# A graph transformer's edge stage: the running maximum moved from TensorE and DVE to DVE alone, q fetched three quads in front, sums added half a quad later

## The chip, the cores and the metric

The kernel runs on one core of one Trainium2 chip. The metric is the device time of one execution in microseconds. Engines: TensorE (PE), VectorE (DVE), ScalarE (ACT), GpSimd (POOL) and SyncE (SP), each with a queue of its own that runs in order; they meet in semaphores. POOL's gathers and scatters are indirect DMAs whose descriptors POOL makes itself; SP issues the plain ones.

## The reference

Two layers of a heterogeneous graph transformer on 6250 nodes, 100000 edges sorted by destination, 8 heads of 16, 16 node types and 32 edge types; then a projection, a residual and a layer norm. What matters here is the step over the edges:

```python
kw = kT[src, :, etype]                       # rows of a table with one entry per (node, edge type)
m = vT[src, :, etype]
a = jnp.einsum('ehd,ehd->eh', kw, q[dst]) * pri[:, etype].T / SQRT_D
amax = jax.ops.segment_max(a, dst, num_segments=n)
ex = jnp.exp(a - amax[dst])
att = ex / jax.ops.segment_sum(ex, dst, num_segments=n)[dst]
hag = jax.ops.segment_sum((m * att[:, :, None]).reshape(-1, H * HS), dst, num_segments=n)
```

## The kernel before, in words

A layer has a stage that builds (`fused`) and one over the edges (`attend`). The first makes, for each tile of 128 nodes, q, k and v and from them `relation_table`, 32 rows of 256 words (key and value) a node, and stores it in HBM. Before it in the first layer, a preparation sorts the nodes by type, spreads the edges over slots, and stores the per-slot flags (`segment_flags`, -1e30 at a segment's edge and 0 elsewhere) and the destination places (`edge_places`).

The edge stage works on 26 blocks of 32 slots; a slot holds 128 edges (one a partition) of one destination tile of 128 nodes. Four slots are a quad, so a block has 8 quads, and each engine runs a loop of one `step` per quad. What a quad X goes through, in steps:

- POOL gathers its rows, 4 indirect DMAs of 128 rows of 1 KB (L795), into a ring of three blocks. Two waits hold it back: TensorE's sums of the quad 24 places before must be done, and q of quad X - LEAD (10) - 1 computed.
- SP loads the destination places of the 512 edges to all partitions (`load_places`, L610), ring of 4, and once a block the flags (`load_flags`, L603), two loads.
- DVE compares places with the partition number (`turned`, L1752), two steps ahead: a one-hot matrix, two buffers. TensorE multiplies it by the resident q (`fetch_q`, L1270), one step ahead, into banks 1 and 2 in turn.
- Step X: DVE multiplies rows by q (L1744) and sums by head to scores (L1757).
- In the steps of the next block the maxima of the whole block are found (`find_maxima`, below).
- Step X+12: DVE weights the messages by the exponentials (`weigh`, L1766), ACT makes another one-hot (`mark`, L1014 and L1017, ring of 3). Step X+13: TensorE sums the slots (`sum_quad`, L1283, banks 5, 6, 7 and 0). Step X+14: DVE adds the four sums of 136 columns into `sums`, the resident totals by tile (`add`, L1781).

The running maximum. An edge's maximum is that over all edges of its destination. DVE adds the masks (L1800); TensorE turns the block so that a partition holds a chunk of 256 consecutive edges of one head (L1313); DVE scans forward and backward (L1812, L1815), where a flag of -1e30 breaks the run, and scans the flags themselves (L1806, L1808). TensorE takes the ends of the 16 chunks to one row (L1321), DVE copies (L1822) and scans along that row (L1827, L1829) and copies back (L1833, L1834), TensorE turns the carries to a column (L1327), DVE copies them (L1838) and takes the maximum with what lies in the chunk (L1841, L1844), TensorE turns back (L1334), DVE subtracts (L1850) and ACT takes the exponential (L1025). Where a block begins inside a segment, the total so far is rescaled: TensorE spreads the factors (L1297), DVE multiplies (L1790, L1792). In `find_maxima` a pair (q, place) says behind which of the four adds of which step a piece stands. On TensorE the same steps hold `sum_quad`, then `fetch_q`, then the piece of the maximum.

After the last gather of the second layer POOL stores `sums` by indirect DMAs (L805), first the tiles that are complete.

## Time and profile before

| | us |
|---|---|
| three runs | 4201.57, 4218.53, 4223.54 (median 4218.53) |
| profiled execution, first to last instruction | 4190.3 |
| PE busy | 2425.6 (58%) |
| DVE busy | 2714.8 (65%) |
| ACT busy | 1707.4 (41%) |
| POOL busy | 2540.4 (61%) |

The page gives the span of the profiled execution and no other time for it. Busy shares are averages over the building stages (0 to about 640 and 1950 to 2620 us), the edge stages (640 to 1950 and 2620 to 3990 us) and the last projection. Waits are put down to the engine that released them; "remote" (or "another core or an unknown queue") is a wait whose releaser the profile can't name, "issue" one in which it shows nothing to wait for. The starts of PE's instructions are recorded, their ends modelled.

### The profile page before, as it was taken

The page shows a single profiled execution, that of the slowest core. Times are in us where ns is not written, and L with a number is a line of the kernel's source. Part 1 is how long each engine was busy: PE and PEld are TensorE (multiplying, and loading weights), DVE is VectorE, ACT ScalarE, POOL GpSimd, SP SyncE. Part 2 cuts the span into 40 slices and gives each one's busy share as a digit, 9 for nine tenths or more (in the row PEclk, how much of TensorE's full clock was granted, in tenths as well). Part 3 has the DMA queues.
Part 4 walks back from the last instruction along what each step waited for, and adds up shares of the span by engine and source line. Part 5 has one row for each costly group of instructions (what it writes and reads, how often), then busy time and mean ns, then how long its engine had stood idle before and what let it go on. Part 6 is the DMA issues. An engine that isn't in the chain of part 4 may idle for free.

```text
span 4190.3 us, 54460 instructions
## 1 busy us (share of the span) xinstructions
PE 2425.6 (58%) x12785; PEld 1767.6 (42%) x12786; DVE 2714.8 (65%) x6706; ACT 1707.4 (41%) x3970; POOL 2540.4 (61%) x2596
## 2 busy tenths in 40 slices
PE   3777771455555556556677777145555555555355
PEld 2333331355445555455333333144544444444343
DVE  7666662566666666667778877156766667666465
ACT  3666660233223333324566666022333333223255
POOL 4666556666666666661566664666666666666426
PEclk8899885677777777776799888577777777777666
DMA  8999984344444444444799997444444444444131
GB/s 202 406 412 409 417 356 136 110 118 123 123 117 117 120 119 120 116 115 109 249 382 375 409 390 326 131 114 117 116 114 113 113 113 112 114 113 114 51 112 48
DMA packets 321826, 782.64 MB, mean 187 GB/s; under 512 B 87083, under 2 KB 249803, under 8 KB 309007
## 3 DMA queue, kind: packets, MB, share of 16 engines
q0 software_dynamic: 110672, 651.37, 44.2%
q1 hardware_dynamic: 202387, 127.10, 11.7%
q8 instruction: 126, 2.06, 0.2%
q10 hardware_dynamic: 8448, 0.53, 0.1%
q14 instruction: 193, 1.58, 0.1%
HBM read 335.58 MB, written 573.46 MB: 217 GB/s over the span
## 4 chain that ended last, share of the span: by engine, by line
DVE 19%; issue 19%; PE 18%; DMA 16%; another core or an unknown queue 16%; ACT 5%; DVEq 4%; POOL 3%; SPq 0%; POOLq 0%; ACTq 0%
DMA relation_table<-region,scatter_node 14%; PE bank L1283 6%; DVE sums L1781 6%; PE bank L1270 4%; PE bank L1116 3%; ACT region L878 3%; DVE region L1766 2%; DVEq L1770 1%; DVE region L1744 1%; DVEq L1781 1%; DVE region_q L1752 1%; PE bank L1146 1%; PE bank L1321 1%; DVEq L396 1%
## 5 line engine op out<-in xcount | busy, mean ns | idle before, releaser
L795 POOL DMA_INDIRECT region<-relation_table,key_of x1664 | 1634.6, 982 | 886.5 <-issue 461.9
L1283 PE MATMUL bank<-region,arena 128*128 128x136 f32 x3328 | 694.3, 371 | 514.5 <-DVE region L1766 298.4
L1014 ACT ACTIVATE arena<-iota_free,minus_dst 128x128 f32<-128x128 f32 x1664 | 528.4, 388 | 831.7 <-remote 433.9
L1283 PEld LDWEIGHTS bank<-region,arena 128*128 128x128 f32 x3328 | 600.6, 262 | 594.6 <-DVE sums L1781 290.0
L1744 DVE TENSOR_TENSOR region<-bank,region 128x512 f32<-128x512 f32 x416 | 285.1, 685 | 871.2 <-remote 670.3
L1116 PE MATMUL bank<-sums,arena 128*128 128x512 bf16 x2048 | 630.7, 418 | 244.0 <-ACT region L878 212.2
L878 ACT COPY region<-bank 128x512 f32<-128x512 f32 x1152 | 624.4, 601 | 359.9 <-DMA relation_table<-region,scatter_node 220.9
L1570 DVE COPY region<-bank 128x512 f32<-128x512 f32 x896 | 585.5, 685 | 264.7 <-DMA relation_table<-region,scatter_node 173.5
L1270 PE MATMUL bank<-region_q 128*128 x3328 | 604.5, 342 | 187.9 <-issue 99.4
L1270 PEld LDWEIGHTS bank<-region_q 128*128 128x128 f32 x3328 | 570.8, 257 | 201.7 <-issue 201.2
L1781 DVE TENSOR_TENSOR sums<-sums,bank 128x136 f32 x1664 | 473.6, 285 | 78.7 <-DVE sums L1781 29.9
L1025 ACT ACTIVATE region<-arena 128x256 f32<-128x256 f32 x52 | 21.7, 417 | 1031.4 <-DVE arena L1850 789.2
L1116 PEld LDWEIGHTS bank<-sums,arena 128*128 128x128 bf16 x2048 | 197.0, 103 | 577.1 <-ACT region L878 295.8
L1766 DVE TENSOR_TENSOR region<-region 128x512 f32<-128x512 f32 x416 | 284.0, 683 | 2.1
L1757 DVE TENSOR_REDUCE arena<-region 128x32 f32<-128x512 f32 x416 | 280.4, 674 | 0.1
L1017 ACT ACTIVATE arena<-arena 128x512 f32<-128x512 f32 x416 | 262.0, 630 | 13.1
L718 POOL TENSOR_TENSOR sums<-arena,sums 128x256 f32<-128x256 f32 x128 | 86.1, 673 | 266.2 <-ACT arena L896 262.7
L1752 DVE TENSOR_SCALAR region_q<-arena,row_no 128x512 f32<-128x512 bf16 x416 | 206.9, 497 | 13.8 <-issue 7.3
L1577 DVE COPY arena<-bank 128x1024 bf16<-128x1024 bf16 x256 | 175.4, 685 | 49.9 <-issue 14.1
L1137 PE MATMUL bank<-identb,sums 128*128 128x128 bf16 x2048 | 176.2, 236 | 4.1 <-POOL sums L722 4.1
L1137 PEld LDWEIGHTS bank<-identb,sums 128*128 128x128 bf16 x2048 | 152.9, 107 | 58.5 <-issue 18.4
L735 POOL DMA_INDIRECT relation_table<-region,scatter_node x128 | 128.9, 1007 | 73.6 <-issue 33.3
(243 smaller groups left out, 2655.3 us busy)
## 6 DMA issues: line engine op xcount, KB each, us to landing
arena<-edge_places SPq DMA_DIRECT2D x416, 128.0 KB
region<-relation_table,key_of POOLq DMA_INDIRECT x1664
arena<-segment_flags SPq DMA_DIRECT2D x104, 128.0 KB
region_q<-q_rows SPq DMA_DIRECT2D x6, 768.0 KB, 6.5
aggregated_rows<-one_less_alpha SPq DMA_DIRECT2D x17, 256.0 KB
region<-aggregated_rows SPq DMA_DIRECT2D x16, 272.0 KB, 3.0
sums<-relation_weight_parts SPq DMA_DIRECT2D x32, 128.0 KB
x_sorted<-arena SPq DMA_DIRECT2D x16, 256.0 KB
```

The lines of the kernel that those rows point to most:

```text
L795: pool.indirect_dma_start(out=rows[:, block_.r, q * QUAD + s], out_offset=None, in_=table, in_offset=bass.IndirectOffsetOnAxis(ap=key_of[: ...
L878: nc.scalar.copy(stage[:, r, :, k * HS:(k + 1) * HS], bank[TABLE_BANK + k % TABLE_BANKS][:, :].rearrange("p (t o) -> p t o", t=RT)).then_i ...
L1014: chain.step(nc.scalar.activation(onehots[:, at, s], iota_free[:, :], ACT.Abs, bias=minus_dst[:, bass.ds(block_.b * BLOCK + (q * QUAD + s) ...
L1116: nc.tensor.matmul(bank[TABLE_BANK + k % TABLE_BANKS][:, :], x_spreadT[:, k, :], w_rel[:, k, :], start=True, stop=True).then_inc(table_psu ...
L1137: ins = nc.tensor.transpose(bank[SPREAD_BANK[half]][:, :].bitcast(BF16)[:, k * P:(k + 1) * P], x_spread[:, tile.par, half * H + k].rearran ...
L1270: ins = nc.tensor.matmul(bank[1 + q % 2][:, s * D:(s + 1) * D], onehotT[:, q % 2, s], q_rows[:, bass.ds(tiles[s], 1), :].rearrange("p a n ...
L1283: ins = nc.tensor.matmul(bank[SUM_BANK[q % 2][pair]][:, s * SUMC:(s + 1) * SUMC], onehots[:, at, 2 * pair + s], rows[:, block_.r, slot, RH ...
L1570: v.tensor_copy(stage[:, r, :, k * HS:(k + 1) * HS], bank[TABLE_BANK + k % TABLE_BANKS][:, :].rearrange("p (t o) -> p t o", t=RT)).then_in ...
L1744: v.tensor_tensor(here, bank[1 + q % 2][:, :].rearrange("p (s d) -> p s d", s=QUAD), here, ALU.mult).then_inc(prod_ready, 1)
L1757: v.tensor_reduce(score[:, block_.par, q * QUAD:(q + 1) * QUAD, :], rows[:, block_.r, q * QUAD:(q + 1) * QUAD, 0:D].rearrange("p s (h o) - ...
L1766: v.tensor_tensor(msg, msg, bc(part[:, :, RHS0:D], 3, HS), ALU.mult).then_inc(weighted, 1)
L1781: v.tensor_tensor(total, total, bank[SUM_BANK[q % 2][n // 2]][:, (n % 2) * SUMC:(n % 2 + 1) * SUMC], ALU.add).then_inc(sum_added, 1)
```

## The change

- The maximum is found on DVE alone. DVE's transpose works on squares of 32x32, so a block is turned in 32 squares: a partition then holds, for one of 4 strips of slots and one head, 8 runs of 32 consecutive edges. Runs are scanned both ways (flags at the runs' edges always break), their ends copied to 32 partitions, scanned along a strip, turned, scanned along a row over the strips, turned back, scanned again, and put in as seeds at the runs' ends; then the runs are scanned both ways once more and turned back.
- q is fetched three quads in front, in banks 1 to 4 (bank 3 and 4 were the maximum's); four one-hot buffers, DVE's comparison 4 steps ahead. On TensorE `fetch_q` stands ahead of `sum_quad`. LEAD is 12.
- DVE adds the first two slots of a quad in step X+14 behind its middle, the other two in step X+15. The rescaling's factors come with the first sum into the same bank. ACT's one-hot ring is 4.
- SP loads the flags in 12 pieces a block, behind the places of quad 3. In the preparation DVE makes the runs' flags, and SP stores 6 arrays instead of 2.

```diff
-LEAD = 10
+LEAD = 12
 FIRST_SUMMED = FIRST_WEIGHED + 1
-FIRST_ADDED = FIRST_SUMMED + 1
+FIRST_ADDED = FIRST_SUMMED + 2
...
-ONEHOT_RING, DST_RING = 3, 4
+ONEHOT_RING, DST_RING = 4, 4
+Q_BANK = (1, 2, 3, 4)
+Q_AHEAD = len(Q_BANK) - 1
+SQUARE = 32
+RUNS = P // SQUARE
+STRIPS = SQUARE // H
+STRIP = BLOCK // STRIPS
+ROW_PLACES = STRIPS + 2
...
+            sp.wait_ge(breaks_ready, 2)
             for k in range(2):
-                sp.dma_start(flag_rows[k].rearrange("(c p) e -> p c e", p=P), s_flag[:, k]).then_inc(flags_stored, 16)
+                sp.dma_start(flag_rows[k].rearrange("r (p e) -> p r e", p=P),
+                             s_flag[:, k].rearrange("p c (g e) -> p (c g) e", g=RUNS)).then_inc(flags_stored, 16)
+            for k in range(4):
+                sp.dma_start(run_rows[:, k].rearrange("c (p g) -> p c g", p=P), s_runs[:, k]).then_inc(flags_stored, 16)
...
+        column, part = divmod(2 * i + par, P // BLOCK)
         for k in range(2):
-            rows_ = flag_rows[k, bass.ds((2 * i + par) * BLOCK, BLOCK), :]
-            source = bc(rows_.rearrange("(j i) e -> j (i e)", i=PER_CHUNK), 1, H)
-            sp.dma_start(flags[:, par, k, :], source).then_inc(flags_in[par], 16)
+            for g in range(RUNS):
+                strips = flag_rows[k, column * RUNS + g, part * BLOCK * SQUARE:(part + 1) * BLOCK * SQUARE].rearrange("(x e) -> x e", x=STRIPS)
+                sp.dma_start(flags[g * SQUARE:(g + 1) * SQUARE, par, k, :], bc(strips, 1, H)).then_inc(flags_in[par], 16)
+        runs = run_rows[column, :, part * BLOCK * RUNS:(part + 1) * BLOCK * RUNS].rearrange("k (x r) -> x k r", x=STRIPS)
+        for k in range(4):
+            sp.dma_start(run_flags[:, par, k, :], bc(runs[:, k], 1, H)).then_inc(flags_in[par], 16)
...
-            wait(sp, scans_ready, b + (l * NBLOCKS - 1))
-            load_flags(i, par)
             for q in range(QPB):
                 load_places(i, par, q)
+                if q == DST_RING - 1:
+                    wait(sp, scans_ready, b + (l * NBLOCKS - 1))
+                    load_flags(i, par)
...
-        wait(pe, prod_ready, quad - 1)
+        wait(pe, prod_ready, quad - Q_AHEAD)
+        at = q_place(block_, q)
         for s in range(QUAD):
-            ins = nc.tensor.matmul(bank[1 + q % 2][:, s * D:(s + 1) * D], onehotT[:, q % 2, s],
+            ins = nc.tensor.matmul(bank[Q_BANK[at]][:, s * D:(s + 1) * D], onehotT[:, at, s],
                                    q_rows[:, bass.ds(tiles[s], 1), :].rearrange("p a n -> p (a n)"), start=True, stop=True)
         ins.then_inc(q_psum, 1)
...
-            wait(pe, sum_added, 4 * quad + (2 * pair - 6))
+            into = bank[SUM_BANK[pair_place(block_, q, pair)]]
+            wait(pe, sum_added, 4 * quad + 2 * (pair + 1 - len(SUM_BANK)))
+            if q == 0 and pair == 0:
+                pe.wait_ge(cross_ready, block_.b + (l * NBLOCKS + 1))
+                nc.tensor.matmul(into[:, 2 * SUMC:2 * SUMC + H], cross_hot[:, :], lower[:, :], start=True, stop=True)
             for s in range(2):
                 slot = q * QUAD + 2 * pair + s
-                ins = nc.tensor.matmul(bank[SUM_BANK[q % 2][pair]][:, s * SUMC:(s + 1) * SUMC], onehots[:, at, 2 * pair + s],
+                ins = nc.tensor.matmul(into[:, s * SUMC:(s + 1) * SUMC], onehots[:, at, 2 * pair + s],
                                        rows[:, block_.r, slot, RHS0:TABLE_ROW], start=True, stop=True)
             ins.then_inc(sum_psum, 1)
...
-            nc.tensor.matmul(bank[4][:, 0:H], cross_hot[:, :], lower[:, :], start=True, stop=True).then_inc(rescale_psum, 1)
+        if block_.real:
+            if q % 2 == 0:
+                tiles = slot_tiles(block_.b, q + Q_AHEAD)
+            coming = ahead(block_, q, Q_AHEAD)
+            if coming[0].real:
+                fetch_q(*coming, tiles[QUAD * (q % 2):])
         late = late_quad(block_, q, FIRST_SUMMED)
         if late[0].real:
             sum_quad(*late)
...
+    by_strip = lambda ap: ap.rearrange("p (b x h) -> p x b h", x=STRIPS, h=H)
+    run_edges = lambda ap: ap.rearrange("p (b e) -> p e b", e=SQUARE)
+
     def find_maxima(block_, q, place):
         b, old, half = block_.b + 1, block_.par, block_.half
         before = b + (l * NBLOCKS - 1)
+        breaks, passes = flags[:, old], run_flags[:, old]
         if (q, place) == (0, 0):
             dve.wait_ge(score_ready, b * QPB + l * NQUADS)
+            chain.step(v.tensor_tensor(by_strip(masked), score[:, old].rearrange("p (x b) h -> p x b h", x=STRIPS),
+                                       bc(invalid[:, bass.ds(b * BLOCK - BLOCK, BLOCK)].rearrange("p (x b) -> p x b", x=STRIPS), 3, H),
+                                       ALU.add))
         if (q, place) == (0, 1):
+            chain.wait()
+            chain.step(v.transpose(turned_max, masked))
+        if (q, place) == (0, 2):
+            dve.wait_ge(flags_in[old], half * FLAG_LOADS + FLAG_LOADS * (l * NBLOCKS // 2 + 1))
+            chain.wait()
+            chain.step(v.tensor_tensor_scan(fwd[:, :], breaks[:, 0, :], turned_max, -BIG, ALU.add, ALU.max))
         if (q, place) == (0, 3):
+            chain.wait()
+            chain.step(v.tensor_tensor_scan(bwd[:, ::-1], breaks[:, 1, ::-1], fwd[:, ::-1], -BIG, ALU.add, ALU.max))
         if (q, place) == (1, 0):
+            chain.wait()
+            into = run_max[:, :, :].rearrange("p k (b g) -> p k b g", g=RUNS)
+            for g in range(RUNS):
+                chain.step(v.tensor_copy(into[:, :, :, g], run_edges(bwd[g * SQUARE:(g + 1) * SQUARE])[:, ::1 - SQUARE, :]))
+            chain.step(v.tensor_reduce(strip_ends[:, 2:4, 0], passes[:, 0:2, :], AX.X, ALU.min))
         if (q, place) == (1, 1):
             chain.wait()
+            chain.step(v.tensor_tensor_scan(strip_ends[:, 0, ::-1], passes[:, 0, :], run_max[:, 0, :], -BIG, ALU.add, ALU.max))
+            chain.step(v.tensor_tensor_scan(strip_ends[:, 1, ::-1], passes[:, 1, ::-1], run_max[:, 1, ::-1], -BIG, ALU.add, ALU.max))
+        if (q, place) == (1, 2):
+            chain.wait()
+            chain.step(v.transpose(end_rows[:, :], strip_ends[:, :, :].rearrange("p k e -> p (k e)")))
+        if (q, place) == (1, 3):
+            chain.wait()
+            chain.step(v.tensor_copy(row_in[0:1, :, :, 1:1 + STRIPS], end_rows[0:1, :].rearrange("o (k x h) -> o k h x", k=4, h=H)))
+            chain.step(v.tensor_copy(row_in[0:1, 0, :, 0], carried[:, :]))
         if (q, place) == (2, 0):
+            row = lambda k: row_in[0:1, k].rearrange("o h s -> o (h s)")
+            chain.wait()
+            chain.step(v.tensor_tensor_scan(row_out[0:1, 0:H * ROW_PLACES], row(2), row(0), -BIG, ALU.add, ALU.max))
+            chain.step(v.tensor_tensor_scan(row_out[0:1, H * ROW_PLACES:2 * H * ROW_PLACES][:, ::-1], row(3)[:, ::-1], row(1)[:, ::-1],
+                                            -BIG, ALU.add, ALU.max))
         if (q, place) == (2, 1):
             chain.wait()
+            both = row_out[0:1, :].rearrange("o (k n) -> o k n", k=2)[:, :, 0:H * ROW_PLACES]
+            chain.step(v.tensor_copy(row_back[0:1, :].rearrange("o (k x h) -> o k h x", k=2, h=H),
+                                     both.rearrange("o k (h s) -> o k h s", h=H)[:, :, :, 0:STRIPS]))
         if (q, place) == (2, 2):
             chain.wait()
+            chain.step(v.transpose(strip_carry[:, :], row_back[:, :]))
+        if (q, place) == (2, 3):
+            chain.wait()
+            chain.step(v.tensor_copy(run_carry[:, 0:2 * SQUARE + 2:2 * SQUARE + 1], strip_carry[:, ::SQUARE]))
+            chain.step(v.tensor_tensor_scan(run_carry[:, 1:SQUARE + 1], passes[:, 0, :], run_max[:, 0, :], strip_carry[:, 0:1],
+                                            ALU.add, ALU.max))
+            chain.step(v.tensor_tensor_scan(run_carry[:, SQUARE + 1:2 * SQUARE + 1][:, ::-1], passes[:, 1, ::-1], run_max[:, 1, ::-1],
+                                            strip_carry[:, SQUARE:SQUARE + 1], ALU.add, ALU.max))
+
         if (q, place) == (3, 0):
+            chain.wait()
+            into_run = run_carry[:, :].rearrange("p (k n) -> p k n", k=2)[:, :, 0:SQUARE]
+            chain.step(v.tensor_tensor(run_seed[:, :, :], into_run, passes[:, 2:4, :], ALU.add))
+            chain.wait()
+            seeds = run_seed[:, :, :].rearrange("p k (b g) -> p k b g", g=RUNS)
+            for g in range(RUNS):
+                chain.step(v.tensor_copy(end_seed[g * SQUARE:(g + 1) * SQUARE], seeds[:, :, :, g]))
         if (q, place) == (3, 1):
             chain.wait()
+            ends = run_edges(bwd)[:, ::SQUARE - 1, :]
+            chain.step(v.tensor_tensor(ends, ends, end_seed[:, :, :], ALU.max))
         if (q, place) == (3, 2):
             chain.wait()
+            chain.step(v.tensor_tensor_scan(fwd[:, :], breaks[:, 0, :], bwd[:, :], -BIG, ALU.add, ALU.max))
+        if (q, place) == (3, 3):
+            chain.wait()
+            v.tensor_tensor_scan(bwd[:, ::-1], breaks[:, 1, ::-1], fwd[:, ::-1], -BIG, ALU.add, ALU.max).then_inc(scans_ready, 1)
         if (q, place) == (4, 0):
+            dve.wait_ge(scans_ready, before + 1)
+            chain.step(v.transpose(turned_max, bwd))
+            chain.wait()
+            v.tensor_tensor(below_max[:, :, :].rearrange("p (x b) h -> p x b h", x=STRIPS), by_strip(masked), by_strip(turned_max),
                             ALU.subtract).then_inc(below_ready, 1)
+            chain.step(v.tensor_tensor(lower[:, :], row_in[0:1, 0, :, 0], turned_max[0:1, 0:H], ALU.subtract))
+            v.tensor_copy(carried[:, :], row_out[0:1, 0:H * ROW_PLACES].rearrange("o (h s) -> o h s", h=H)[:, :, STRIPS])
             v.tensor_scalar(cross_hot[:, :], iota_free[0:1, :], crossing[:, bass.ds(b - 1, 1)], None, ALU.is_equal)
         if (q, place) == (4, 1):
             chain.wait()
...
-        late, weigh_next = late_quad(block_, q, FIRST_ADDED), late_quad(block_, q, FIRST_WEIGHED)
-        adding, before = late[0].real, block_.shift(-1)
-        if adding:
-            tiles = slot_tiles(late[0].b, late[1])
+        older, newer = late_quad(block_, q, FIRST_ADDED), late_quad(block_, q, FIRST_ADDED - 1)
+        weigh_next, before = late_quad(block_, q, FIRST_WEIGHED), block_.shift(-1)
+        if older[0].real:
+            tiles = slot_tiles(older[0].b, older[1] * QUAD + QUAD // 2)
+        elif newer[0].real:
+            tiles = [None] * (QUAD // 2) + list(slot_tiles(newer[0].b, newer[1] * QUAD))
         if block_.real:
             multiply(block_, q)
-        if adding and q == FIRST_ADDED:
-            scale_crossing(before.b, tiles)
         weigh_place = 0 if not block_.real and q != FIRST_WEIGHED else 3
         for place in range(4):
             if place == 0 and weigh_place == 0 and weigh_next[0].real:
                 weigh(*weigh_next)
-            if adding:
-                add(late[0].b, late[1], place, tiles)
-            coming = ahead(block_, q, 2)
+            if place < QUAD // 2 and older[0].real:
+                add(*older, place + QUAD // 2, tiles[place])
+            if place >= QUAD // 2 and newer[0].real:
+                if newer[1] == 0 and place == QUAD // 2:
+                    scale_crossing(newer[0], tiles[place])
+                add(*newer, place - QUAD // 2, tiles[place])
+            coming = ahead(block_, q, Q_AHEAD + 1)
             if place == 0 and coming[0].real:
                 turned(*coming)
             if place == 1 and block_.real:
```

## Rows read from the trace of the kernel before

**Rows 1.** By stage: us; PE, PEld, DVE, ACT, POOL busy (count); clock, DMA, GB/s

```profile
0.00:640.00 640.00, 429.90 (x2345) 214.21 (x2346) 434.06 (x704) 390.62 (x728) 379.37 (x401) 0.89 0.93 363
...
1904.00:1934.00 30.00, 20.45 (x134) 17.75 (x132) 27.80 (x80) 13.39 (x39) 0.00 (x0) 0.92 0.05 13
800.00:1850.00 1050.00, 601.91 (x3178) 530.39 (x3178) 699.34 (x1919) 334.55 (x910) 680.94 (x693) 0.74 0.44 119
```

**Rows 2.** The product with q alone: its starts in three stretches (layer start, steady, GpSimd silent)

```profile
L1744 DVE TENSOR_TENSOR region<-bank,region x9: 675/691/692, 650.0 to 740.4; 128x512 f32<-128x512 f32 x9
...
L1744 DVE TENSOR_TENSOR region<-bank,region x174: 659/692/693, 801.2 to 1846.7; 128x512 f32<-128x512 f32 x174
...
L1744 DVE TENSOR_TENSOR region<-bank,region x8: 665/684/692, 1904.8 to 1934.2; 128x512 f32<-128x512 f32 x8
```

**Rows 3.** Groups by line, DVE and GpSimd, 800 to 1850 us; last row 646 to 701 us

```profile
L1744 DVE TENSOR_TENSOR region<-bank,region 128x512 f32<-128x512 f32 x174 | 119.4, 686 | 293.4 <-remote 202.0 <-PE bank L1270 58.7 <-issue 32.0
L1822 DVE COPY carry_in<-bank 1x256 f32<-1x256 f32 x44 | 16.2, 404 | 9.0 <-remote 8.1 <-PE bank L1321 0.8
L1808 DVE TENSOR_TENSOR_SCAN arena<-arena 128x256 f32<-128x256 f32 x22 | 15.1, 685 | 0.0
...
L1844 DVE SCALAR_TENSOR_TENSOR arena<-arena,chunk_carry 128x256 f32<-128x256 f32 x22 | 10.4, 472 | 0.0
L1827 DVE TENSOR_TENSOR_SCAN carry_out<-carry_in 1x136 f32<-1x136 f32 x22 | 9.3, 421 | 0.0
L1800 DVE TENSOR_TENSOR arena<-arena,invalid 128x256 f32<-128x256 f32 x21 | 8.9, 423 | 0.0
L1833 DVE COPY row_words<-carry_out 1x128 f32<-1x128 f32 x22 | 5.8, 266 | 0.0
L1838 DVE COPY chunk_carry<-bank 128x2 f32<-128x2 f32 x22 | 3.2, 148 | 5.9 <-remote 5.9
...
L795 POOL DMA_INDIRECT region<-relation_table,key_of x693 | 683.0, 986 | 369.4 <-issue 188.8 <-remote 97.0 <-PE bank L1283 66.0
...
L795 POOL DMA_INDIRECT region<-relation_table,key_of x45 | 42.7, 949 | 13.7 <-issue 13.7
```

**Rows 4.** Timeline in the middle of the first layer: start, us, engine, what, idle before

```profile
1314.92 1.16 PE L1270 MATMUL bank<-region_q 128*128 x8
...
1319.32 0.94 POOL L795 DMA_INDIRECT region<-relation_table,key_of  x1 [0.30 <-issue]
1322.12 0.69 DVE L1744 TENSOR_TENSOR region<-bank,region 128x512 f32<-128x512 f32 x1 [9.41 <-remote]
1322.34 1.28 ACT L1014 ACTIVATE arena<-iota_free,minus_dst 128x128 f32<-128x128 f32 x4 [6.51 <-remote]
...
1323.01 0.94 POOL L795 DMA_INDIRECT region<-relation_table,key_of  x1 [2.75 <-remote]
```

**Rows 5.** Timeline at the first layer's start

```profile
664.67 2.07 PE L1270 MATMUL bank<-region_q 128*128 x8 [7.30 <-DVE region L1744]
...
679.58 0.69 DVE L1744 TENSOR_TENSOR region<-bank,region 128x512 f32<-128x512 f32 x1 [14.45 <-issue]
...
701.98 0.69 DVE L1744 TENSOR_TENSOR region<-bank,region 128x512 f32<-128x512 f32 x1 [20.72 <-remote]
```

**Rows 6.** Timeline late in the second layer

```profile
3884.59 1.92 PE L1270 MATMUL bank<-region_q 128*128 x8
...
3931.46 0.97 POOL L805 DMA_INDIRECT aggregated_rows<-sums,place_row  x1 [0.30 <-issue]
3937.93 0.69 DVE L1744 TENSOR_TENSOR region<-bank,region 128x512 f32<-128x512 f32 x1 [33.69 <-remote]
```

**Rows 7.** Timeline: stores and loads of flags on SyncE, and DVE's wait for the stores

```profile
73.72 1.23 SPq L574 DMA_DIRECT2D segment_flags<-region  x2
...
91.03 0.06 DVE L1640 MEMSET junk<- 1x1 f32 x1
...
1287.80 1.16 SPq L603 DMA_DIRECT2D arena<-segment_flags  x2
```

More of the change, by code:

```diff
@@ L35 @@
 SCOLS = -(-SLOTS // P)
[L36 to L38 removed]
+CLEN = BLOCK * H
 QUAD = 4
@@ L1344, in attend @@
                 pe.wait_ge(stage_dve, V * TILES * (l + 1))
-                fetch_q(Block(0, 0), 0, slot_tiles(0, 0))
+                for q in range(Q_AHEAD):
+                    if q % 2 == 0:
+                        tiles = slot_tiles(0, q)
+                    fetch_q(Block(0, 0), q, tiles[QUAD * (q % 2):])
                 block_of(Block(0, 0))
@@ L1513, in _ @@
             v.memset(junk2[:, :], 0.0).then_inc(prep_done, 1)
+            by_run = lambda k: s_flag[:, k].rearrange("p c (g e) -> p (c g) e", e=SQUARE)
+            for k, edge in enumerate((0, SQUARE - 1)):
+                chain.step(v.tensor_reduce(s_runs[:, k].rearrange("p c g -> p (c g)"), by_run(k), AX.X, ALU.min))
+                chain.step(v.tensor_copy(s_runs[:, 2 + k].rearrange("p c g -> p (c g)"), by_run(k)[:, :, edge]))
+            chain.wait()
+            for k, edge in enumerate((0, SQUARE - 1)):
+                v.memset(by_run(k)[:, :, edge], -BIG).then_inc(breaks_ready, 1)
             def keep_slots(c):
@@ L1803, in find_maxima @@
                     if (q, place) == (0, 1):
-                        dve.wait_ge(flags_in[old], half * 32 + 32 * (l * NBLOCKS // 2 + 1))
-                        chain.step(v.tensor_tensor_scan(first_seg[:, :], flags[:, old, 0, :], flags[:, old, 0, :], 0.0, ALU.min, ALU.min))
+                        chain.wait()
[4 more added lines that the diff above has]
+                        chain.step(v.tensor_tensor_scan(fwd[:, :], breaks[:, 0, :], turned_max, -BIG, ALU.add, ALU.max))
@@ L1817, in find_maxima @@
-                    if (q, place) == (2, 0):
-                        dve.wait_ge(chunk_rows, before + 1)
-                        got = bank[4][0:1, :].rearrange("o (k h j) -> o k h j", k=4, h=H)
-                        for n in range(2):
-                            at = 1 - n
-                            chain.step(v.tensor_copy(carry_in[0:1, n, :, :, at:at + CHUNKS], got[:, 2 * n:2 * n + 2]))
-                        chain.step(v.tensor_copy(carry_in[0:1, 0, 0, :, 0], carried[:, :]))
+                        chain.step(v.tensor_tensor_scan(strip_ends[:, 0, ::-1], passes[:, 0, :], run_max[:, 0, :], -BIG, ALU.add, ALU.max))
@@ L1896, in attend @@
                 link(v.memset(sums[:, :, :], 0.0))
-                for q in range(2):
+                for q in range(Q_AHEAD + 1):
                     turned(Block(0, 0), q)
```

145 lines of the change are left out of this document (47 added, 98 removed).

## The prediction

> **What bounds the kernel now.** I read the table by stage first, then the groups by line, then the timeline where an engine waits longest. Each of the two layers has a stage that builds the relation table and a stage that goes through the edges in 26 blocks of 8 quads. The building stages have the DMA engines 93% busy [rows 1] and hold no code that the change rewrites. So the question is the edge stages. In them DVE is the busiest compute engine, and yet it idles: 699.34 of 1050 us are busy [rows 1]. The starts of its product with q (L1744, once a quad) give the pace: 173 steps from 801.2 to 1846.7 us are 6.04 us a quad, 48.35 us a block [rows 2]. 1050 us are then 21.7 blocks, and DVE idles (1050 - 699.34) / 21.7 = 16.2 us in each.
>
> Nearly all of that idle time (293.4 us of 351) stands before L1744 [rows 3], 202.0 us of it with a releaser that the profile can't name. That instruction waits for two things: gathered rows and q from TensorE. The timeline tells which. At 1312.7 us DVE falls idle. The q that it waits for and the one after it are computed by 1314.92 + 1.16 = 1316.08 us, but DVE goes on at 1322.12, ScalarE (which waits for TensorE's sums) at 1322.34 and GpSimd (which waits for TensorE too) at 1323.01 [rows 4]. Three engines go on together, 6 us after TensorE's recorded end: TensorE's results are seen late. It is worst where GpSimd issues gathers without a break. At the start of a layer q is computed at 664.67 to 666.74 us, and DVE, which takes one quad at 679.58, takes the next only at 701.98 [rows 5]: 35 us late. There GpSimd issues 45 gathers in 55 us and waits for nothing [rows 3]. Late in the second layer it issues the stores of the sums back to back: q computed at 3884.59 to 3886.51 us is used at 3937.93, after DVE stood idle for 33.69 us; the last store was issued at 3931.46 [rows 6]. And where GpSimd is silent (1904 to 1934 us) the lateness is gone: 7 steps take 29.4 us, 33.6 us a block, DVE is busy 27.80 of 30 us [rows 1, 2]. So a block costs DVE 33.6 us of own pace, and some 15 us of late TensorE results.
>
> The second bound is GpSimd: 693 gathers have 683.0 us busy and 188.8 us of issue [rows 3], 1.258 us each, 32 x 1.258 = 40.3 us a block, whatever the other engines do. The other 8 us of the 48.35 it waits for TensorE.
>
> **The change part by part.**
>
> *The maximum on DVE alone.* Four trips DVE - TensorE - DVE per block go: for the turned scores, the chunk ends, the carry, the turned maxima. DVE's idle time in front of the instructions that take these results is small: 9.0 us before L1822 and 5.9 before L1838 [rows 3], under 1 us a block together with the two of the same kind that I don't show. But TensorE's queue is in order: while it waits for the carry or the maxima, the next q product stands behind, and that share is hidden in L1744's wait. TensorE loses some 4 us of work a block, which is on nobody's path.
>
> DVE's instructions: 11 go. Two scans at 0.685, two copies of 256 at 0.404, two row scans at 0.421, two copies at 0.266, one at 0.148, two scalar-tensor operations at 0.472 [rows 3] are 4.6 us. 26 come. Two long scans are 1.37 us. Two transposes of 128x256 have no row: between 0.42 (L1800, elementwise on as many) and 0.685 (a scan); I take 0.42, since a transpose carries no running value, 0.84 us. 19 instructions on 2 to 64 columns lie between 0.148 (L1838) and 0.266 (L1833, 128 columns); I take 0.18, 3.4 us. A copy of 128 and two small transposes are 0.74 us. Together 6.35 us, net +1.7, and +0.2 for two places where DVE waits for its own instruction just before: **+1.9 us a block**. With neighbours overlapping it may be 0.9, with the upper durations 4.0. They all stand on DVE's in-order stream, so they are on the path: DVE's own pace becomes 33.6 + 1.9 = 35.5 us.
>
> The Trainium skill (VectorE: DVE Perf Modes, Rules for kernel authors) speaks against this part: since each chained DVE operation drains, one is to minimise the count of operations, not the semaphores. The trace agrees on the fixed part (a copy of 2 columns takes 148 ns); by that rule alone the 15 more instructions cost 15 x 0.148 = 2.2 us a block, and the change would be slower, which is the first rival below. For the long transposes the same skill (Vector Engine (DVE) Microarchitecture Reference, The reshape front-end and per-opcode configuration) gives one element per cycle per lane, an estimate of 0.27 us plus the fixed part; no row shows it.
>
> *q three quads in front, in four banks.* Before, q of quad Q is computed during step Q-1 and DVE needs it at the start of step Q, with about 1 us to spare. After, three steps lie between, 3 x 4.4 = 13 us. Of the 174 in the steady stretch 97 wait; their 293.4 us [rows 3] are 3.0 us each in the mean and 9.4 at most, which is the one in [rows 4]. Lateness of this size is covered wholly. Nothing is added but SBUF and an order of instructions: the lookahead costs DVE the same one-hot comparison, only earlier.
>
> *The adds half a quad later, TensorE fetching q before summing.* The weighting of a quad ends step X+12, TensorE sums in about 2.2 us, DVE adds at the start of step X+14 before and in its middle after. The slack rises from some 2.5 to some 4.5 us. This is what stays: the sums' results are as late as q's, and 4.5 us doesn't cover the long ones. The four one-quad buffers of one-hots give ScalarE a quad more.
>
> *Flags.* SyncE issues 12 loads a block in place of 2, which take 1.16 us for two [rows 7], so some 7 us; they now stand between the places of quads 3 and 4. Those of quad 4 are needed 4 steps (17 us) after their buffer is free: hidden; if not, DVE waits some us a block. In the first building stage the stores of flags and run rows are 6 for 2, in pieces of 128 and 16 bytes. They are issued at 73.72 us and DVE needs them at 91.03 [rows 7]: 17 us cover them. I take 0, at most +10. The added reduces and copies there fall into DVE's idle time before L1577 at 73 us.
>
> **The sum.** DVE's own pace 35.5 us. Of its 16.2 us of idle time all before L1744 is coverable, but the adds inherit a part: with a mean lateness of 3.0 + 1 us and 4.5 us of slack, I let a bit under half go, 7.3 us, and 8.9 us stay. I don't take more, as GpSimd will be busier (40.3 of 44.4 us, not of 48.35) and [rows 5] shows what steady gathers do. Block: 35.5 + 8.9 = **44.4 us**, 4.0 less. 48 blocks beyond each layer's first two: -192 us. The first 8 quads take 90.4 us [rows 2] where GpSimd streams; with three q's per release of TensorE's results I take 20 us less per layer, -40 (0 to -45 each). The profiled span 4190.3 becomes 3958. The page has no time beside the span; the three runs lie 11 to 33 us above it, their median 28.2 (4218.53). 4218.5 - 232 = **3986 us**, its own range 3900 to 4065.
>
> **The rivals.**
> 1. *The sums take q's place (slower).* GpSimd alone ends the lateness (it pauses when TensorE's sums don't come, 1319.32 to 1323.01 in [rows 4]), so the waits move to L1781 at unchanged length, and DVE's 1.9 us come on top. This decides if the lateness after a weighting is over 4.5 us as a rule. For it: the three engines were released together. Against it: the mean of 3.0 us. 52 x 1.9 = 99, flags +8: 4325 us. Chance 0.14.
> 2. *All lateness is covered.* DVE at 35.5 us, GpSimd's 40.3 us bound: 8.05 x 48 + 40 = 426 less, 3792 us. Against it: GpSimd without pauses is the state of [rows 5]. Chance 0.12.
> 3. *A quarter of the idle time goes* (4 us): 48.35 + 1.9 - 4 = 46.25, 101 + 40 less, 4077 us. Chance 0.16.
> 4. *It cancels*: what the lookahead brings, DVE's upper price (4.0 us) takes: 4218 us. Chance 0.07.
>
> Forecast 0.51. Faster by over 0.5% (21 us, the spread of the three runs): 0.51 + 0.12 + 0.16 = 0.79; within 0.07; slower 0.14. The range 3790 to 4230 holds all but the first rival.
>
> **What would show it.** L1744's line: idle time before it falls from 14 us a block to under 3; the adds' line rises from 1 to 4 to 7 us. DVE's busy time a block 32 to 34, transposes at 0.42, the stretch where GpSimd is silent at 35.5 us a block. GpSimd's waits 8 to 4 us. First product to the ninth 70 us, not 90. Wrong would be: waits of the adds over 10 us a block, a SyncE load as releaser of the one-hot comparison, or transposes over 0.7 us.

## The result, and the profile after

The changed kernel takes 4258.3 us (median of 4 runs, 4252.4 to 4265.2), the kernel before 4216.2 beside it: ratio 1.0101, interval 1.0083 to 1.0119. It is 1% slower where 5.5% faster was forecast. The profiled execution spans 4263.4 us, 73.1 more than that of before. The medians are only 42.1 us apart: the profiled execution of the changed kernel is the slowest of its four (4265.2 us), and that of before spans 11 us less than its fastest timed run takes. So some 31 us of the 73.1 are the spread of executions and not the change.

The table by stage of the changed kernel, the 1050 us that answer to the last of [rows 1] (us; PE, PEld, DVE, ACT, POOL busy; clock; DMA; GB/s):

```profile
800.00:1850.00 1050.00, 587.27 (x2800) 513.83 (x2800) 734.89 (x2196) 336.02 (x909) 671.58 (x680) 0.70 0.42 117
```

The product with q in its first nine quads and in the steady stretch, which answers to [rows 2]:

```profile
L1756 DVE TENSOR_TENSOR region<-bank,region x9: 675/691/693, 667.2 to 771.6; 128x512 f32<-128x512 f32 x9
...
L1756 DVE TENSOR_TENSOR region<-bank,region x177: 653/692/693, 860.9 to 1939.8; 128x512 f32<-128x512 f32 x177
```

176 steps in 1078.9 us are 49.0 us a block, 48.3 before; the first eight quads take 104.4 us, 90.4 before. The groups by line, 800 to 1850 us, which answer to [rows 3] (L1756 is the product, L1793 the adds, L1299 and L1316 TensorE's `fetch_q` and `sum_quad`):

```profile
L1793 DVE TENSOR_TENSOR sums<-sums,bank 128x136 f32 x682 | 194.2, 285 | 160.8 <-issue 97.0 <-remote 31.2 <-PE bank L1316 18.7
L1756 DVE TENSOR_TENSOR region<-bank,region 128x512 f32<-128x512 f32 x172 | 117.8, 685 | 79.1 <-issue 68.5 <-remote 5.6 <-PE bank L1316 2.3
L1821 DVE STREAM_TRANSPOSE arena<-arena 128x256 f32<-128x256 f32 x22 | 9.5, 433 | 0.0
L1834 DVE COPY arena<-arena 32x16 f32<-32x16 f32 x84 | 17.4, 207 | 2.4 <-remote 0.2 <-issue 0.2
...
L823 POOL DMA_INDIRECT region<-relation_table,key_of x680 | 671.6, 988 | 382.5 <-issue 185.5 <-remote 97.1 <-PE bank L1316 70.3
```

The waits did move. 293.4 us before the product [rows 3] have become 79.1, and 160.8 stand before the adds. GpSimd's line has hardly changed: 988 ns a gather, and 167 us of waits for TensorE's sums and for releasers without a name (97.1 + 70.3) against 163 [rows 3]. A round of it looks as before too. A part of the timeline of the changed kernel:

```profile
1387.34 0.48 DVE L1764 TENSOR_SCALAR region_q<-arena,row_no 128x512 f32<-128x512 bf16 x1
...
1390.86 0.30 DVE L1793 TENSOR_TENSOR sums<-sums,bank 128x136 f32 x1 [1.61 <-issue]
1393.00 0.30 DVE L1793 TENSOR_TENSOR sums<-sums,bank 128x136 f32 x1 [1.84 <-issue]
1397.23 0.69 DVE L1756 TENSOR_TENSOR region<-bank,region 128x512 f32<-128x512 f32 x1 [3.33 <-issue]
...
1399.70 1.28 ACT L1042 ACTIVATE arena<-iota_free,minus_dst 128x128 f32<-128x128 f32 x4 [6.19 <-remote]
1400.38 0.94 POOL L823 DMA_INDIRECT region<-relation_table,key_of  x1 [3.15 <-remote]
```

GpSimd issued 12 gathers from 1381.8 to 1397.2 us, paused 3.15 us, and only then did the others go on. From 1388.7 to 1399.3 us most of the small register and semaphore instructions between DVE's operations take 0.70 us each, not 0.06; that is the "issue" of these rows.

Where GpSimd is silent, behind the last gather of layer 1, the changed kernel takes 35.5 us for 8 quads, against 33.5 before (1900.7 to 1934.2 us):

```profile
L1756 DVE TENSOR_TENSOR region<-bank,region x9: 660/692/693, 1936.2 to 1971.7; 128x512 f32<-128x512 f32 x9
```

Where the 73.1 us are, from the starts of the gathers, products and adds in the two timelines: preparation and first building +18.1; the 832 gathers of layer 1 +23.8 and of layer 2 +16.1; last gather to last product -4.4 and +1.2; last product to last add +13.4 and +9.9; second building -5.0; the end 0.0. The 39.9 us in the gathers are not to be laid to the change: in later runs on a chip of this kind the repaired kernel (e9, below) is only 0.2% slower than the kernel before beside it, and its gathers take still longer (1277.0 and 1282.2 us, against 1275.2 and 1272.5 here and 1251.4 and 1256.4 in the profile of before). The first building and the two ends together, 41.4 us, are as much as the medians differ.

The first term is on SyncE. Its queue in the changed kernel, against [rows 7]:

```profile
74.20 3.66 SPq L594 DMA_DIRECT2D run_breaks<-region  x2
77.90 4.55 SPq L597 DMA_DIRECT2D run_flag_rows<-region  x4
...
83.94 41.26 SPq L545 DMA_DIRECT2D arena<-in_L_gnn_Watt_dram  x8
```

Issuing these eight loads took 4.97 us in the kernel before; here 41.26, behind the six stores in small pieces, and a further 22.71 for the next eight. The store of the third group of nodes (`x_sorted`) stands behind these and eight loads more, and is issued at 151.8 us in place of 101.2. The building stage runs dry meanwhile: between 130 and 150 us TensorE is busy 2.80 us, 13.63 before. e7, below, tests this.

Another term is in DVE's register loads: each quad, DVE loads four tile numbers for the adds. The loads of the kernel before, then of the changed one, over the whole trace (min/median/max ns):

```profile
L1770 DVEq TENSOR_LOAD <-dst_tile x416: 278/343/1109, 775.6 to 4007.8; - x139
```

```profile
L1782 DVEq TENSOR_LOAD <-dst_tile x418: 4/964/3758, 799.8 to 4081.4; - x140
```

The load now begins at the third slot of a quad, and takes 964 ns. DVE's product stands behind it in DVE's queue.

### The profile page after: what moved, and what is told of

Read it like the earlier page. It is cut to its first block and busy times, and to the rows that moved or that the text cites. A ratio compares the mean times of both kernels' runs of the same rounds, so it can differ in the third digit from the quotient of the medians.

```text
span 4263.4 us, 54391 instructions
## 1 busy us (share of the span) xinstructions
PE 2449.7 (57%) x11863; PEld 1800.2 (42%) x11954; DVE 2839.9 (67%) x7495; ACT 1712.2 (40%) x3970; POOL 2543.4 (60%) x2596
## 5 line engine op out<-in xcount | busy, mean ns | idle before, releaser
L1316 PE MATMUL bank<-region,arena 128*128 128x136 f32 x3328 | 844.1, 400 | 943.0 <-DVE sums L1793 469.1
L1316 PEld LDWEIGHTS bank<-region,arena 128*128 128x128 f32 x3328 | 666.3, 276 | 1087.8 <-DVE sums L1793 595.8
L1299 PE MATMUL bank<-region_q 128*128 x3328 | 697.1, 375 | 311.4 <-issue 175.9
L1299 PEld LDWEIGHTS bank<-region_q 128*128 128x128 f32 x3328 | 630.3, 280 | 342.1 <-issue 334.3
L1144 PE MATMUL bank<-sums,arena 128*128 128x512 bf16 x1958 | 610.3, 420 | 284.4 <-ACT region L906 176.9
L1793 DVE TENSOR_TENSOR sums<-sums,bank 128x136 f32 x1664 | 475.0, 285 | 430.0 <-issue 191.9
L1756 DVE TENSOR_TENSOR region<-bank,region 128x512 f32<-128x512 f32 x416 | 285.0, 685 | 326.8 <-issue 183.7
L763 POOL DMA_INDIRECT relation_table<-region,scatter_node x128 | 129.1, 1009 | 73.5 <-issue 33.7
```

The lines of the kernel that those rows point to most:

```text
L1144: nc.tensor.matmul(bank[TABLE_BANK + k % TABLE_BANKS][:, :], x_spreadT[:, k, :], w_rel[:, k, :], start=True, stop=True).then_inc(table_psu ...
L1299: ins = nc.tensor.matmul(bank[Q_BANK[at]][:, s * D:(s + 1) * D], onehotT[:, at, s], q_rows[:, bass.ds(tiles[s], 1), :].rearrange("p a n -> ...
L1316: ins = nc.tensor.matmul(into[:, s * SUMC:(s + 1) * SUMC], onehots[:, at, 2 * pair + s], rows[:, block_.r, slot, RHS0:TABLE_ROW], start=Tr ...
L1756: v.tensor_tensor(here, bank[Q_BANK[q_place(block_, q)]][:, :].rearrange("p (s d) -> p s d", s=QUAD), here, ALU.mult).then_inc(prod_ready, 1)
L1793: v.tensor_tensor(total, total, bank[SUM_BANK[pair_place(block_, q, n // 2)]][:, (n % 2) * SUMC:(n % 2 + 1) * SUMC], ALU.add).then_inc(sum ...
```

## The experiments

Theory G: GpSimd sets the pace of the edge stage with its gathers, and with the pauses in which TensorE's results get through; DVE is not the bound. Theory D is the prediction's own reading: DVE's chain with TensorE's latencies is the bound, and GpSimd has 8 us a block to spare. Each run stands beside the kernel before on the same chip, and a ratio is always against the same chip. The chips are of two kinds. On two of them (e1 to e4, and e5 to e8) the kernel before takes 3715 to 3718 us, on a third (e9 to e12) 4222 us, about as where the pair was measured. The expectations of e1 to e4 were written for the slower kind and ran on the faster, so their totals in us can't be compared, and the paces of a block only in part.

**e1, e2: half of the gathers.** `for s in range(QUAD)` becomes `range(2)` behind the first three blocks, in either kernel.

> The kernel before, with 2 of the 4 gathers of every quad behind the first three blocks left out (the rows of the other two slots stay what they were, so the output is not the reference's). GpSimd then needs some 20 us a block in place of 40.3. Theory G (the gathers set the pace: while GpSimd issues them without a break TensorE's results are seen late, GpSimd itself then waits for such a result, and only its pause of some 3 us lets everything go on; 40.3 us of gathers and 8.4 us of pauses are the block's 48.3): the long waits of DVE go, and a block takes DVE's own pace, 33.6 to 36 us; some 3550 to 3650 us. Theory D (DVE's chain of product, weighting and sums with TensorE's latencies sets the pace, GpSimd's pauses only follow it): a block stays above 44 us, over 4000 us.

> The changed kernel with the same half of the gathers left out. It measures the own pace of what is not gathers, to be set beside the same of the kernel before. Theory G: 35 to 38 us a block, 1 to 3 us more than the kernel before shows in its run, since DVE carries 2.3 us more work and a register load of 0.96 in place of 0.34 us a quad. Theory D: above 44 us.

3379.2 us (0.909 of the kernel before) and 3536.3 us (0.952). The products of the two runs:

```profile
L1745 DVE TENSOR_TENSOR region<-bank,region x161: 659/684/692, 770.7 to 1457.8; 128x512 f32<-128x512 f32 x161
```

```profile
L1757 DVE TENSOR_TENSOR region<-bank,region x161: 658/692/693, 788.3 to 1534.1; 128x512 f32<-128x512 f32 x161
```

160 steps are 20 blocks: 34.4 and 37.3 us (34.5 and 36.9 in layer 2), both in the range that theory G gave. With fewer gathers DVE's own pace shows, and the change makes it 2.4 to 2.9 us longer; DVE's busy time went from 31.6 to 33.6 us a block. But this chip was of the faster kind, where DVE hardly waits for TensorE (e8, below), so it could not yet speak for the pair's.

**e3, e12: more work on DVE.** In the kernel before:

```diff
+                    chain.step(v.tensor_scalar(flat, edge_places[:, q % DST_RING], row_no[:, 0:1], None, ALU.is_equal))
+                    chain.wait()
                     v.tensor_scalar(flat, edge_places[:, q % DST_RING], row_no[:, 0:1], None, ALU.is_equal).then_inc(onehotT_ready, 1)
```

> The kernel before with DVE's one-hot comparison done twice in every quad (0.50 us each, the second one waits for the first, so some 0.55 us a quad, 4.4 us a block on DVE's queue; the values are the same). Theory G: DVE's work is not on the path while its pace (33.6 + 4.4 = 38 us) is below the gathers' 48.3: the block stays within 0.8 us, below 4260 us. Theory D: every microsecond on DVE's queue counts: 48.3 + 4.4 = 52.7 us a block, 4220 + 52 x 4.4 = 4450 us.

> The kernel before with DVE's one-hot comparison done twice again (some 4.0 us more busy time a block on DVE's queue), meant for a chip on which the kernel before takes 4220 us. Theory G (a round of 12 gathers and a pause of GpSimd sets the pace there, whatever DVE has to do): the block stays at 48 to 49.5 us and the kernel below 4270 us. Theory D: 52.5 us a block, 4430 us. On a chip where the kernel before takes 3715 us: 3694 us as measured.

On the faster kind of chip 3694.3 us, ratio 0.994 (0.992 to 0.997): 0.6% faster with 4 us more work a block. I can't explain it. The gathers last 974 ns there against 989 in e8, but that is another chip. On the slower kind 4244.0 us, ratio 1.005 (1.003 to 1.007): 0.4 us a block over the whole, where theory D wanted 4.0 to 4.4. The steady blocks of that profile take 49.7 and 49.8 us in the two layers, a little above theory G's 49.5; in the profile of before the same 20 blocks take 48.5 and 48.8 (from the runs of the pair, and an execution well under its median). So of 3.8 us more busy time a block between a tenth and a third shows. Where GpSimd is silent all of it shows, 37.6 us for 8 quads against 33.5:

```profile
L1744 DVE TENSOR_TENSOR region<-bank,region x9: 666/684/692, 1923.4 to 1961.0; 128x512 f32<-128x512 f32 x9
```

DVE's work does not set the pace while GpSimd gathers, on either kind of chip.

**e4, e11: breaks for GpSimd.** In the kernel before, behind every quad's gathers:

```diff
+                    for _ in range(2):
+                        chain.wait()
+                        chain.step(nc.gpsimd.memset(rest[:, :], 0.0))
```

> The kernel before with two small memsets, each waiting for the last, on GpSimd behind the four gathers of every quad: a break of some 0.4 to 0.6 us in the stream of gathers, 3 to 5 us a block. Theory G: if short breaks let TensorE's results through, the long pauses (8.4 us a block) go, the block takes 40.3 + 4 = 44 to 46 us and the kernel 4050 to 4130 us. If they don't, the breaks add to the pauses: 48.3 to 52 us a block, 4220 to 4420 us. Theory D: no change, 4220 us, as GpSimd has 8 us to spare a block.

> The kernel before with the two small memsets on GpSimd behind every quad's gathers again, this time meant for a chip on which the kernel before takes 4220 us and GpSimd pauses 8.4 us a block for late TensorE results. It cost 4.6 us a block where the gathers never paused (46.0 us a block, 3963 us). If short breaks let the results through, GpSimd's long pauses go and the block takes 46 to 46.5 us here too: 4060 to 4110 us, 3% faster than before. If only pauses of 2 us or more do, the breaks add up: 50 to 53 us a block, 4320 to 4450 us. On a chip where the kernel before takes 3715 us: 3963 us as measured.

On the faster kind 3963.2 us, ratio 1.067 (1.065 to 1.069): 45.9 us a block, 4.5 more than in e8, so there GpSimd alone is the bound (theory D had no change). On the slower kind 4191.5 us, ratio 0.991 (0.989 to 0.994); neither branch of the expectation. The gaps of over 0.45 us between gathers are 9.9 us a block in the steady part of layer 1 (5.6 of them breaks of 0.9 to 1.2 us), against 8.3 in the profile of before, and the block takes 48.5 against 48.3. So 5.6 us of breaks cost next to nothing: long pauses give way to short ones. Theory G did not foresee this. The gain is at the layers' starts. The first eight quads take 42.7 and 43.3 us in place of 90.4 and 90.1, the next eight 95.2 and 64.3 in place of 55.9 and 53.9; layer 1 gives most of it back (8 us stay), layer 2 keeps 36 us.

**e5, e8: the pair on the faster kind of chip**, unchanged.

> The changed kernel as it is, beside the kernel before on the same chip. The kernel before took 4216 us where the pair was measured and 3715 us on the chip of the first four experiments, where GpSimd's gathers alone set a block's pace (40.8 us). On a chip of that second kind DVE's own pace (37.1 us in the changed kernel) stays under the gathers, so both theories give the same steady pace, and only the 17 us lost in the preparation and some 10 us at the ends are left: ratio 1.006 to 1.011. On a chip of the first kind: ratio 1.010 again.

> The kernel before as it is, for its profile on this chip. If the block takes 40.8 us here, as GpSimd's 32 gathers need, DVE's idle time (16 us a block where the pair was measured) falls to about 8 us and TensorE's results are seen at once; a time of 3715 us. If the chip is of the first kind: 48.3 us a block and 4216 us.

3754.1 against 3718.1 us, ratio 1.0101 (1.0084 to 1.0118), the same as of the pair; the kernel before again 3716.3. GpSimd and DVE of the kernel before, 800 to 1600 us:

```profile
L795 POOL DMA_INDIRECT region<-relation_table,key_of x620 | 613.1, 989 | 189.0 <-issue 182.0 <-PE bank L1270 4.3 <-PE bank L1283 2.7
```

```profile
L1744 DVE TENSOR_TENSOR region<-bank,region 128x512 f32<-128x512 f32 x154 | 106.2, 690 | 151.2 <-DMA region<-relation_table,key_of 147.6 <-PE bank L1270 3.1
```

and GpSimd of the changed kernel:

```profile
L823 POOL DMA_INDIRECT region<-relation_table,key_of x619 | 613.3, 991 | 188.6 <-issue 176.7 <-PE bank L1316 10.1 <-PE bank L1299 1.8
```

GpSimd hardly waits in either (no gap between gathers is over 0.4 us), a block takes 41.4 us in both, and DVE waits for gathered rows. Nearly the whole loss is at the ends: from the one timeline to the other +11.9 us to the first gather, +12.5 and +10.5 from last product to last add, +6.7 in the gathers; the rest of that profile is 12 us shorter, and its run was the fastest of four (3744.1 us, 10 under the median). The ratio, 1.0101, is at the upper end of the forecast's 1.006 to 1.011.

**e6, e7, e9: two repairs of the changed kernel.** A second table of tile numbers that begins two entries on, and the flags' stores on ScalarE's queue:

```diff
-                        tiles = slot_tiles(older[0].b, older[1] * QUAD + QUAD // 2)
+                        tiles = slot_tiles(older[0].b, older[1] * QUAD, from_third)
...
-                            sp.dma_start(run_rows[:, k].rearrange("c (p g) -> p c g", p=P), s_runs[:, k]).then_inc(flags_stored, 16)
+                            act.dma_start(run_rows[:, k].rearrange("c (p g) -> p c g", p=P), s_runs[:, k]).then_inc(flags_stored, 16)
```

> The changed kernel with DVE's register load of four tile numbers taken from a second table that begins two entries further on, so that it starts at a multiple of four entries as in the kernel before. If the place inside the table is what makes the load last 0.96 us, it lasts 0.34 us again: 0.62 us a quad, 5 us a block less on DVE's register part. Where the gathers set the pace (theory G) the time stays within 15 us of the changed kernel's; if DVE's queue set it (theory D), 52 x 3 us = 150 us less (the idle time of 3.1 us a block before the product goes). If the load still lasts 0.96 us, the place is not the cause.

> The changed kernel with the six stores of flags issued by ScalarE's queue at the start of its first tile in place of SyncE's. If SyncE's queue, full of small pieces, is what holds the loads behind it (41 us for eight loads in place of 5) and with them the second group's store, the first product with q comes at 650 to 656 us in place of 667 and the kernel is 10 to 17 us faster than the changed one. If the small pieces hold up the DMA engines themselves, whatever queue they are in, it stays at 667 us.

> The changed kernel with both repairs: DVE's register load from the second table, and the stores of flags on ScalarE's queue. On a chip where the gathers follow each other without a pause, the two account for the whole loss apart from the change's longer work on DVE behind the last product: 3754 - 17 (stores) - 18 (two drains at 10 and 9 us, from the product to the last add) = 3719 us, ratio 1.000 to 1.003 to the kernel before. Were the loss elsewhere, the ratio would stay above 1.005. On a chip where GpSimd pauses 8 us a block (where the pair was measured), some 35 us under the changed kernel as well, if not more, ratio about 1.002.

e6: 3739.7 us, ratio 1.006 (1.004 to 1.008), 14 less than e5. The load is back at its old length, so its place in the table is the cause:

```profile
L1787 DVEq TENSOR_LOAD <-dst_tile x418: 337/343/1499, 736.0 to 3547.8; - x140
```

From last product to last add it takes 45.1 and 43.2 us, 55.1 and 52.2 in e5 and 42.6 and 41.7 in e8. e7: 3736.7 us, ratio 1.005 (1.003 to 1.007), 17 less than e5; the first product comes at 653.7 us and not at 662.9, and the third group's store is issued at 123.9 us. In the kernel before (e8) the first product comes at 652.3. e9, both, on the slower kind of chip: 4231.4 us, ratio 1.002 (1.001 to 1.003), as forecast (about 1.002). Set against the 1.0101 of the pair, as the changed kernel did not run on that chip, these two are 0.8 of the 1.0%. Its drain and that of the changed kernel, from last product to last add in layer 1:

```profile
1959.10:2003.50 44.40, 30.85 (x114) 24.68 (x114) 34.41 (x117) 21.53 (x60) 0.00 (x0) 0.60 0.39 100
```

```profile
1971.70:2028.20 56.50, 34.00 (x114) 26.96 (x114) 34.83 (x116) 20.88 (x58) 0.00 (x0) 0.50 0.31 78
```

DVE is as busy in both (34.4 and 34.8 us); the 12 us between them are its idle time, which goes with the load (e6). Behind the last gather e9 takes 33.7 us for 8 quads, where the changed kernel takes 35.5 and the kernel before 33.5. And e9's steady blocks take 49.2 us, the changed kernel's 49.0: the load costs nothing while GpSimd gathers.

**e10: half of the gathers and the aligned load.**

> The changed kernel with half of the gathers left out behind the first three blocks, and with the aligned register load. It splits the 2.8 us by which DVE's own pace was longer in the changed kernel (37.1 against 34.4 us a block, both without the other half of the gathers): if the load's 0.62 us a quad stands on the path only in front of the product (3.1 us of idle time a block there in the changed kernel, and its busy time is 2.0 us longer), the block falls to 34.5 to 36 us; if the load is hidden while DVE is never waited for, it stays at 37.

3577.7 us, on the slower kind of chip (0.847 of the kernel before there):

```profile
L1762 DVE TENSOR_TENSOR region<-bank,region x161: 651/671/692, 842.0 to 1538.4; 128x512 f32<-128x512 f32 x161
```

34.8 us a block, in the forecast's 34.5 to 36. So on the slower kind of chip too the steady lateness goes with the gathers, and half of them let DVE run at its own pace. Against e2 (37.3) the load was worth some 2 us of it, and against e1 (34.4) next to nothing is left of the change's price, though DVE is busy 33.3 us a block against 31.6: its idle time is 1.5 against 2.7 us. The chips differ, so these are no clean differences; the stretches behind the last gather say the same (e9 33.7, changed kernel 35.5, kernel before 33.5). Only the first eight quads stay at 104.8 us: there the first three blocks' gathers are whole.

Leaving out gathers takes away their bytes as well as GpSimd's instructions, and no run separates the two. Two readings speak for the instructions: the short breaks of e11 let the first eight quads through, and in the building stage of the kernel before, between 200 and 600 us, the DMA engines are 99% busy (413 GB/s, against 119 in the edge stage [rows 1]) and no wait for TensorE is over 2.0 us.

## Why the prediction was wrong

**What bounds the kernel.** This step failed. I took DVE's idle time before the product as the slack and GpSimd's 40.3 us as a second bound with 8 us to spare: "The other 8 us of the 48.35 it waits for TensorE". Those 8 us were no room. GpSimd's waits for TensorE are themselves waits for late results, which get through when it pauses; the lookahead changed neither the gathers nor those pauses. In 22 steady blocks of layer 1 the gaps of over 0.45 us are 8.3 us a block before and 8.7 after, and what is left of the block, 40.0 and 40.3 us, is gathers back to back. e12 shows that DVE's work is hardly on this path (0.4 of 4 us), e10 that the gathers are. By how much the pauses could shrink is not settled by this: e11 put 5.6 us of breaks into a block, and it took no longer. That GpSimd's own stream makes the results late I had written down; I then let DVE have the gain of it as though GpSimd did not wait for the same results.

**The idle time.** DVE's own pace was forecast at 35.5 us, and 8.9 us of idle time were to stay. The own pace was right: 35.5 us where GpSimd is silent (with half the gathers 36.9 to 37.3 in e2, on the other kind of chip). But 14.7 us of idle time stayed of 16.1, not 8.9; this is the term of the sum that failed. The product's share fell from 13.7 to 3.6 us (under 3 was foretold), the adds' rose from 1.3 to 7.6 (4 to 7), and what was left over went to other instructions of DVE. At a pace set by GpSimd idle time can only move.

**The maximum's price.** +1.7 us of work and 0.2 of waits forecast, +2.3 measured in busy time (32.1 to 34.4 us a block; 31.6 to 33.6 without the other gathers), transposes 0.433 us against 0.42. The work was priced right, but it is not on the path while gathers run. Where they don't, the pace agrees with the +1.9 (33.5 to 35.5 us) by luck: there it is nearly all the register load, which the prediction left out, and with the aligned load it is 33.7. That the lookahead pays for the rest of the work fits the idle time of e10, and is not tested alone. The Trainium skill (VectorE: DVE Perf Modes, Rules for kernel authors) asks for fewer operations; the prediction's estimate from that rule, 2.2 us for 15 more, is near the busy time that the trace shows, and the kernel's time does not follow it.

**What I didn't price.** The register load: I followed the adds and not the load in front of them. 0.62 us a quad, hidden while gathers set the pace, 10 and 9 us in the two drains on the faster kind of chip (e6). Together with the longer work behind the last product that is +23 us of the two profiles' 73.

**Flags.** "I take 0, at most +10": +18.1 us in the pair's profile, 11.9 on the other chip. I asked when the stores are needed and not what stands behind them in SyncE's queue: 24 loads, and behind these the third group's store. With the stores on ScalarE's queue (e7) the first product comes 9.2 us earlier.

**The layer's start.** 90.4 us did not become 70, but 104.4, though the next eight quads take 37.5 in place of 55.9: together -4. Three q's in front do not help while GpSimd streams. It streams longer, too: its first pause stands behind 64 gathers before (LEAD 10) and behind 72 in the changed kernel (LEAD 12), 71.8 and 82.6 us after the first product. In both this is the gather that waits for the sixth q, by the code. That the eight more gathers make up the 14 us is not tested.

**The rivals.** The first was the closest: the sign, and that the waits move to the adds. Its price (1.9 us on each of 52 blocks, 4325 us) was wrong for the same reason as the forecast, as it too had DVE on the path. Rival 2's state, blocks at GpSimd's own pace, is what the faster chips do in both kernels, before the change as after it. They take 41.4 us, not 40.3: the prediction's sum leaves out the 0.3 us that also stand in front of a gather that waited for something. A gather is 0.986 us and 0.30 us to the next, 41.2 us for 32.

**Open.** Why results are late on one kind of chip and not on the other; DMA packets last about the same on both (those of 4096 bytes 232 and 229 ns in the mean over the kernel before). Whether gathers make results late by GpSimd's instructions or by their bytes. Why short breaks take the place of the long pauses (e11). And why the doubled comparison made e3 faster.

## What to carry to other kernels

A pause of the engine that feeds the rest is room only if what it waits for is not itself delayed by it: take the feeder's work and its pauses together as one bound until a run shows otherwise, and test it by halving its work before working on its consumers. Idle time that all lies before one instruction says where an engine waits; here a lookahead only moved it. Compare medians before laying the difference of two profiles to a change: here 31 of 73 us were the spread of executions. Of every step that is moved follow also the small things: the register load in front of it, and what stands behind its DMAs in the same queue.

## What the hardware showed

- Two kinds of chips: the same kernel takes 3716 us on one and 4222 us on another, nearly all of the difference in the edge stages. The first eight quads of a layer take 39 us on the one and 90 on the other. What sets the chips apart is not known.
- On the slower kind not only are TensorE's results late while gathers follow each other without a pause: in the changed kernel many of DVE's register and semaphore instructions then last 0.70 us. The instructions that make an add's address, in the changed kernel there and on the faster kind (min/median/max ns):

```profile
L1793 DVEq FUSED_REGOPS  x682: 4/57/1410, 861.0 to 1938.6; - x171
```

```profile
L1793 DVEq FUSED_REGOPS  x620: 57/57/64, 787.0 to 1611.7; - x155
```

  Without the register loads, DVE had 320 register and semaphore instructions of 0.6 us or more in the edge stages of the changed kernel and 366 in e9. In the kernel before on a chip of the same kind there were 5, in e12 13, in e11 1, and with half the gathers (e10) 2. Why it takes the changed kernel is open.
- DVE's register load of four words from this table lasts 343 ns where it begins at a multiple of four words of the table, and 964 ns where it begins two words further on (medians; e6 against e5).
- Six stores in pieces of 128 and 16 bytes stretch the issue of the next eight loads of the same queue from 5.0 to 41.3 us; issued by another engine's queue they leave these loads at 8.2 us, though those behind them still slow down.
